# Three moves of issue order in the shared expert of a fused attention and expert kernel: an earlier weight load, a later filler, later scatters

## What is computed

```python
x = x + tanh(g_xattn[0]) * xattn(layernorm(x), ctx, ...)
h = layernorm(x)
h = h + attention(rmsnorm(h, w_ln1), ...)          # causal, 16 heads
xn = rmsnorm(h, w_ln2)
# _moe:
shared = mean(experts(xf, sWg, sWu, sWd), axis=1)  # silu(x Wg) * (x Wu) @ Wd
topk_p, topk_i = top_k(softmax(xf @ Wgate + expert_bias), 2)
routed = einsum('ne,nec->nc', comb, experts(xf, Wg, Wu, Wd))   # 8 experts, I = 256
x = x + tanh(g_ffn[0]) * (h + shared + routed)
```

## Time and profile before

| | us |
|---|---|
| median of 3 runs | 2297.93 (2295.79 to 2301.08) |
| the profiled execution | 2299.8 |
| its span, first to last instruction | 2297.9 |
| PE busy | 2103.8 (92% of the span) |
| DVE / ACT / POOL busy | 1493.7 / 1179.0 / 1375.5 |
| granted TensorE clock, mean | 0.969 |

### The profile page before, as it was taken

How to read it: one execution, slowest core, us unless ns; L and a number is a source line. 1 busy time by engine, 2 the same in 40 slices (tenths; PEclk the granted TensorE clock), 3 DMA queues, 4 the chain that set the end, 5 groups by cost and what they waited for, 6 DMA issues and landing times.

```text
span 2297.9 us, 43310 instructions
## 1 busy us (share of the span) xinstructions
PE 2103.8 (92%) x12568; PEld 957.9 (42%) x12569; DVE 1493.7 (65%) x4180; ACT 1179.0 (51%) x2319; POOL 1375.5 (60%) x1450
## 2 busy tenths in 40 slices
PE   2899999999999986799999999999997898999998
PEld 1333333333333321344444444444443444455554
DVE  3688888888888885466565665656554778444443
ACT  3355555555555544255455454545545664555554
POOL 3276777677767776157556665655654476555554
PEclk7999999999999997999999999999998899999999
DMA  5513233232323231635445353544551685766665
GB/s 164 168 51 116 72 104 97 88 111 79 111 72 104 80 121 48 180 93 169 130 138 163 105 162 110 162 135 132 150 168 43 145 189 110 125 113 116 112 110 92
DMA packets 227829, 272.09 MB, mean 118 GB/s; under 512 B 40136, under 2 KB 165820, under 8 KB 227364
## 3 DMA queue, kind: packets, MB, share of 16 engines
q1 hardware_dynamic: 197180, 212.69, 30.8%
q0 software_dynamic: 22752, 47.86, 12.2%
q10 hardware_dynamic: 7704, 9.20, 1.2%
HBM read 161.76 MB, written 86.54 MB: 108 GB/s over the span
## 4 chain that ended last, share of the span: by engine, by line
PE 71%; DVE 7%; DMA 6%; POOL 6%; issue 5%; ACT 3%; SPq 1%; ACTq 0%; POOLq 0%; DVEq 0%
PE a_bank L700 13%; PE a_bank L780 5%; PE a_bank L752 5%; PE b_bank L1498 4%; PE a_bank L765 4%; PE b_bank L1499 4%; PE b_bank L1500 4%; PE c_bank L2620 3%; PE c_bank L2621 3%; PE c_bank L2619 3%; PE b_bank L1578 2%; PE b_bank L1610 2%; PE b_bank L1595 2%; PE b_bank L1596 2%; PE b_bank L1580 2%
## 5 line engine op out<-in xcount | busy, mean ns | idle before, releaser
L504 ACT ACTIVATE a_pt<-a_bank 128x512 f32<-128x512 f32 x512 | 305.6, 597 | 371.3 <-DVE a_bank L611 366.7
L1454 DVE CUSTOM_DVE_ANT_0 b_bank<-b_bank,b_tri 128x256 f32<-128x256 f32 (+3 forms) x512 | 253.2, 497 | 298.9 <-PE b_bank L1596 294.4
L622 DVE CUSTOM_DVE_ANT_0 a_bank<-a_bank,a_strip 128x512 f32<-128x512 f32 x512 | 353.2, 691 | 3.6 <-PE a_bank L765 2.7
L1205 POOL TENSOR_TENSOR b_acc<-b_acc,b_pt 128x256 f32<-128x256 f32 (+2 forms) x384 | 280.7, 753 | 81.9 <-ACT b_pt L1318 71.1
L414 POOL TENSOR_TENSOR a_acc<-a_acc,a_pt 128x512 f32<-128x512 f32 x256 | 317.8, 1277 | 16.0 <-ACT a_pt L504 15.6
L611 DVE TENSOR_TENSOR a_bank<-a_bank,a_band 128x256 f32<-128x256 f32 (+1 forms) x512 | 205.7, 402 | 131.5 <-PE a_bank L752 130.3
L1318 ACT ACTIVATE b_pt<-b_bank 128x256 f32<-128x256 f32 (+2 forms) x384 | 144.6, 383 | 182.7 <-PE b_bank L1580 165.9
L752 PE MATMUL a_bank<-a_q_stack,a_k_stack 128*128 128x512 f16 x512 | 199.4, 390 | 23.4 <-ACT a_pt L504 14.0
L765 PE MATMUL a_bank<-a_k_stack,a_q_stack 97*128 97x512 f16 x512 | 196.7, 384 | 4.8 <-DVE a_low L622 4.7
L2038 POOL DMA_INDIRECT out_dram<-c_z,c_to_row x71 | 112.5, 1585 | 132.7 <-DMA out_dram<-c_z,c_to_row 99.8
L1578 PE MATMUL b_bank<-b_q_stack,b_k_stack 96*128 96x256 f16 (+3 forms) x512 | 157.1, 307 | 13.5 <-ACT b_pt L1318 7.9
(11 more groups left out here) (342 smaller groups left out, 5356.6 us busy)
## 6 DMA issues: line engine op xcount, KB each, us to landing
b_q_stack<-qk_rows SPq DMA_DIRECT2D x192, 128.0 KB, 2.7
a_q_stack<-qk_rows SPq DMA_DIRECT2D x96, 128.0 KB
a_k_stack<-qk_rows SPq DMA_DIRECT2D x96, 128.0 KB
b_k_stack<-qk_rows SPq DMA_DIRECT2D x96, 128.0 KB, 2.6
a_sums<-in_x SPq DMA_DIRECT2D x34, 256.0 KB, 3.1
qk_rows<-a_qk_hi SPq DMA_DIRECT2D x64, 128.0 KB, 1.7
qk_rows<-a_qk_lo SPq DMA_DIRECT2D x64, 128.0 KB, 1.8
out_dram<-a_sums SPq DMA_DIRECT2D x32, 256.0 KB, 2.0
```

The costliest lines, as they stand in the source:

```text
L504: nc.scalar.activation(pt[:, n % SLOTS, :], st_bank[n % 2][:], ACT.Exp).then_inc(exped, 1)
L622: nc.vector.tensor_tensor_reduce(out=max_bank[step % 2][:], in0=max_bank[step % 2][:], in1=strip[:, g * HG + hh, at:at + S], scale=-1.0, s ...
L1205: nc.gpsimd.tensor_tensor(sums_of, sums_of, probs(n), ALU.add).then_inc(pooled, 1)
L1454: nc.vector.tensor_tensor_reduce(out=max_bank[step % 2][:, 0:w], in0=max_bank[step % 2][:, 0:w], in1=tri[:, at:at + w], scale=-1.0, scalar ...
```

## The change

Three edits, all of order. (1) On SP the loads of routed expert 1's weights (`up_weights(1)`, `down_weights(1)`) stand in `pass_c`'s first pieces; a second `yield` in `pass_b`'s body "last" lets SP issue them ahead of the last batch's stores. They still wait till the shared expert's weights are split. (2) On DVE `find_spare` stands behind the low parts of batch 1's input and the first hidden half. (3) On POOL, from batch 2 on, one tile is scattered ahead of the first `low_part` and four behind the second, where it was two, one between the two `low_part`s, and two.

```diff
@@ pass_b, sync, body
                 if kind == "last":
                     residual(b)
+                    yield
@@ pass_c, sync
             sp.dma_start(table, blank_rows).then_inc(blanked, 16)
             yield
+            up_weights(1)
+            down_weights(1)
+            yield
             prior.all_used(sp)
...
             for b in range(B):
-                up_weights(b + 1)
-                down_weights(b + 1)
+                if b:
+                    up_weights(b + 1)
+                    down_weights(b + 1)
@@ pass_c, gpsimd
                 write_records(b)
                 if b > 1:
-                    scatter_some(b, 2)
+                    scatter_some(b, 1)
                 low_part(b, 0)
-                if b > 1:
-                    scatter_some(b, 1)
                 if b + 2 < B:
                     rms(b + 2)
                 low_part(b, 1)
                 if b + 2 == B:
                     write_records(b + 1)
                 if b:
-                    scatter_some(b, 2 if b > 1 else NT)
+                    scatter_some(b, NT)
@@ pass_c, vector
                 if more:
                     settle(b)
-                    if b == 0:
-                        find_spare()
                     low(b + 1, 0)
                     low(b + 1, 1)
...
                 else:
                     low_part(0)
+                if b == 0:
+                    find_spare()
                 up_weights(b + 1)
```

## The result

The changed kernel took 2309.68 us (median of 5, 2308.12 to 2315.83) against 2297.93 (2295.11 to 2301.08): ratio 1.0049, 95% interval 1.0031 to 1.0066. It is slower by 11.75 us, outside the range of the prediction. The profiled execution (2315.8 us, span 2313.9) is the highest of the five; 5.6 us of it lie ahead of batch 0 (its batch 0 starts at 1778.94, before 1773.32; the granted clock stood at its lower level 6.9 us longer up to there). The rest is in the batches.

What follows compares the result with a forecast made beforehand. PE was taken to set the floor of 19.30 us per shared-expert batch, with waits costing clock too. Terms -6.5 - 6.6 + 7.8 + 3.4 + 1.5 = -0.4 us gave 2297.5 us, range 2290 to 2303.

Steps and rivals of the forecast that it cites:

- batch 0: Shared expert's first batch: hidden half, c_h_lo and PE's down come 6.5 us earlier; -6.5 us.
- batch 2: Fewer scatters ahead of c_h_lo remove both PE waits and the low clock: 25.94 becomes 19.30, -6.6 us.
- batches 3 to 5: Eight scatters delay output, input load and weights, so ACT waits: 66.7 us instead of 58.86, +7.8.
- batches 6 and 7: Loop's end: eight scatters ahead of batch 6's output delay the last scatter and the routed experts; +3.4 us.
- Early weights and filler: Batch 0: early load and moved filler together remove DVE's 6.50 us idle time behind ACT's weights wait; -6.5 us.
- the chain of 42.5 us: From c_h_lo to that two batches on, through scatters, output and weights: 42.5 us against 38.6 at the floor.
- rival 2: Batches 3 to 5: loads and output slow each other, longer chain; 2302.7 or 2307.3 us, chance 0.17.
- End of the loop: Batch 6: eight scatters stand ahead of the output, the table is read later, routed experts start +3.4 us.
- rival 3: Routed experts' start: they do not wait for the table, last two terms fall away; 2292.6 us, chance 0.11.
- The clock term: Routed experts' start: PE waits longer before its first turn and its clock falls; +1.5 us.

Runs made afterwards that it cites:

- d2: The changed kernel run again unaltered, on chip 4; 2295.5 us, ratio 0.9985 to the kernel before.
- c3: The kernel before with the new scatter order alone, a second time, on chip 13; 2318.3 us, ratio 1.0084.
- e6: The changed kernel with the output's DMA issued behind the fourth of the eight scatters; 2288.8 us, ratio 0.9954.
- f1: The kernel of d4 run again, on chip 2; 2288.6 us, ratio 0.9951.
- f2: The changed kernel with two small GpSimd power operations on an unread tile between the fourth and fifth scatters, on chip 2; 2306.1 us, ratio 1.0027.
- e5: The changed kernel with a GpSimd memset of an unread tile among the eight scatters; 2307.7 us, ratio 1.0052.
- c1: The kernel before run again unaltered, on chip 13; 2300.7 us (one time).
- d4: The changed kernel, output's DMA behind the fourth scatter in batches 1 to 5, old order in batch 6, z loads behind next gate/up weights; 2287.3 us, ratio 0.9947.

## Why the prediction was wrong

By its steps, with d2 (kind A) and the changed kernel's own trace (kind B) beside each:

| term | forecast | d2 | changed |
|---|---|---|---|
| batch 0 | -6.5 | -6.7 | -8.4 |
| batch 2 | -6.6 | -6.1 | -2.4 |
| batches 3 to 5 | +7.8 | +8.3 | +13.3 |
| batches 6 and 7 | +3.4 | +4.3 | +7.5 |
| sum | -1.9 | -0.3 | +10.0 |

*Early weights and filler.* Right: ACT no longer waits for the weights in batch 0. 24.5 us was usual; 22.8 came with a shorter time at the lower clock (3.4 instead of 6.8 us).

*Batch 2.* Right at 19.8 us where signals are in time. In the changed kernel's trace the second `xt_hi` waits 1.46 us as a transpose is reported 1.7 us late: the gain shrinks to 2.4.

*Batches 3 to 5.* This is the step that failed: the chain of 42.5 us took it for granted that ACT starts `th` 2.79 us into each batch, since it did from batch 1 on in before. The chain is real. In d2 it took 43.4 us from the second `c_h_lo` of batch 1 to that of batch 3 and 42.0 on to batch 5; ACT waits 4.55 us for Wu in batch 3 (forecast 3.9) and 3.30 in batch 5 (1.9), none in batch 4. That the sum came out so near (+8.3 for +7.8) is partly luck: batch 3 stood at full clock (1.00) and paid nothing of the 2.0 us put down for it, 23.5 us for 25.2, and batch 5 took 24.0 for 22.2. But in the measured kernel's trace eight scatters in a row held TensorE's signals, and batches of 23.3 to 24.5 us are so long that the weights come in time. No rival had this; rival 2, the slower one, had ACT waiting longer for Wu, and the trace has it not waiting at all. Longer than forecast by 5.5 us in 3 to 5 and, for the same reason, 4.2 in batch 2.

*End of the loop.* The last scatter is 5.0 us later in batch 7, against 3.4 forecast, and ACT waits for it, so the table does gate (against rival 3). Batch 6 adds 3.1 us to it by late signals.

*The clock term* (+1.5) was not separately seen; the routed experts grew by 0.5 us.

*The skill's rules.* The fit of the Trainium skill (DMA: Bandwidth & Descriptors, Anatomy of one DMA), an estimate of 4.4 us for the output, would have put batches 3 to 5 at 19.3 us each in d2; they are 23.5, 19.7 and 24.0, so the trace's 10.7 was the right price (10.6 in batch 2 of d2). The weights' flight in batch 3's place was 10.1 us in d2, before 8.8: it moved with what ran beside it, as the prediction had it, though no row singles out the scatters.

Of the 14.2 us between the two times, 2309.7 and 2295.5, 10.2 lie in the batches and go with the kind of the run; the rest is not explained. What I could have seen is that before has a row of eight scatters nowhere but at batch 2; what I could not is that its trace was of kind A.

## What to carry to other kernels

Issuing order on GpSimd is paid for by those who wait for other engines: keep rows of indirect DMAs short (four here), and put the DMA on whose landing a load waits in the middle of them, not behind. When an engine starts late and the profile names no releaser, compare the time of the signal with the end of the instruction that gives it before building a story on queues. And measure a change on more than one chip: here the same kernel was 0.15% faster on chip 4 and 0.4 and 0.7% slower on chip 13, while the version with short rows won 0.5% on chips 4 and 2, one of each kind.

## What the runs showed of the hardware

In runs of kind B TensorE's signals come up to 5 us late (4.99 in c3) while GpSimd issues eight indirect DMAs one behind another (10.1 us). Where four are followed by another DMA's issue (e6, f1) or by 2.13 us of other work (f2), those signals are in time for which ACT's first `th` and `xt_hi` wait, and others still come late (up to 2.2 us in batches 3 to 5 of e6 and f1, and once 4.2 in batch 6 of f1). A break of 0.14 us does not help (e5). Before, whose rows are of two to four but for batch 2 and the loop's end, loses nothing by it (c1: 181.0). Behind a row of eight the last late signals of a batch come through in a burst 1.3 us behind the start of the output's issue, at which time POOL is doing copies; earlier ones come singly within the row (1872.28 above), and in e6 one comes with no such DMA near it. In the same runs some 2,000 of 35,800 signals are missing in the records, most of them DMAs', some of other engines. All are missing behind the first scatter: up to it the changed kernel's trace and d2's have 29,048 each. So the records and the signals may suffer from one thing. Missing records alone would not be strange: by the Trainium skill (NOTIFIC — Programmer's Manual, When the ring fills) a full ring of records drops new ones by default, without stalling the engine. That fits the gaps, and does not explain a late signal.

Open: what that thing is; whether it is the chip or its state; and whether an execution that isn't recorded has it. None of this was tried. Nor were the two edits apart by which d4 differs from e6; by batches, 5.4 us came in batch 2, where ACT's wait ahead of the weights' split is gone, and 2.9 in batches 6 and 7 together.
